# An 8-head attention phase: the last pair's product with the values moved to directly behind the next scores

## The chip, the cores and the metric

The kernel runs on one core of one Trainium2 chip. The metric is the device time of one execution in microseconds (us), taken as the median of several runs. One execution of it was recorded by the profiler, and all rows below come from that trace.

## What is computed

The program is a two-layer decoder on x of 16 batches x 256 rows x 512 features. Each of four steps adds to x: a 16-head cross attention (phase a), a ternary feed-forward step (phase b), an 8-head cross attention with heads of 64 features (phase c), and a routed feed-forward step (phase m). The change lies in phase c alone, whose reference is, cut to its core:

```python
q = layernorm(xn, g, b) @ Wq; k, v = split(media @ Wkv)       # xn: x normalised once more before
q, k, v = heads(q) * 64 ** -0.5, heads(k), heads(v)           # 8 heads of 64
sim = einsum('bhid,bhjd->bhij', q, k)
sim = where(media_mask, sim, neg_inf)
attn = softmax(sim)
out = einsum('bhij,bhjd->bhid', attn, v)
x = x + merge(out) @ Wo
```

## The kernel before, in words

All order is written out by hand: each engine has its own program, and the engines meet only at semaphores. Phase c goes through 16 batches; a batch has two **quads** of four heads (q = 0 and 1), a quad two **pairs** of heads, and a pair is one group of 128 output features. Python names carry the prefix `c_` in the trace. Full-precision products are made of fp32r parts: each operand is split into a high part (written by ScalarE) and a low part (VectorE: the bank minus the high part), and three products are added up.

In one quad TensorE goes through four slots j = 0 to 3:

- T_j: `transpose_probs`, four transposes of the probabilities of head j (L1149) into one bank, which VectorE (even j) or ScalarE (odd j) copies out to `pT`.
- behind T_0 only: `scores` of the *next* quad (L1132, 24 matmuls on 64 rows of the array each).
- behind T_1 the product PV of `probs_v` (L1162) for the last pair of the quad before; behind T_2 the PV of this quad's first pair. It is four fp32 matmuls with 64 columns of weights each, and it shows as eight in the trace. Both write the one bank `o_bank`.
- then the **units** of the slot, from `SLOTS`: pieces of the projections of the next batch, and of the output product (L1079 with `c_wo`) of the batch before. For q = 0 they are [tx0, tx1], [k0], [q0], [o0]; for q = 1 [o1], [k1], [q1 and half of v0], [the rest of v0, v1]. tx0 and tx1 turn the normalised rows of the next batch (L1069, four transposes each), k and q are projections (L1093).

The units share two banks of PSUM in turn: a unit's bank is its place in the list of units modulo 2, and `bank_free` lets it start once the unit before it in the bank is out. tx0 and k0 have the same bank, so k0 waits, beside its other operands, at

```python
            pe.wait_ge(lo_done, units.count(SPLIT, v, ve))     # L1045, here with v = "tx0"
```

for the low part of tx0 (`lo_of`, L810, on VectorE), which itself waits for the high part (`hi_of`, L600, on ScalarE), which waits for tx0's transposes.

ScalarE (`quad_of_8` in `scalar`) takes in turn: the exponentials of the next quad's head 0 (`exps`, L652), the high parts of slot 0, the copy of T_1 (L660), the high part of PV (`attn_hi`, L667), the exponentials of head 1, and so on. VectorE (`quad_of_8` in `vector`) has the copy of T_0 (L855), the score maxima of heads 0 and 1 (`scores_out`, L846), the low parts of slot 0, the maxima of head 2, the low part of PV (`attn_lo`, L881), the maxima of head 3, the copy of T_2.

In the last batch of phase c there are no units for a next batch; in their place the next phase, m, turns its weights (L2519) and its first rows (L2487) in the same slots, with high and low parts again on ScalarE (L2174) and VectorE (L2282). A piece of weight may be turned only once the low part of the piece before the last is out.

Phase a is the same function with 16 heads. There `QUADS` is 4, and its PV stands directly behind `scores` already (`PV_AFTER = {0: -1}`); its scores use 32 rows of the array and its PV 32 columns.

Of the kernel before, what the change touches and what calls it, by code (L numbers as in the profile page):

```python
# [145 lines left out]
def attention_phase(nc, ctx, banks, tag, heads, x_in, ctx_in, mask_in, mask_value, x_out, w_views, q_bias, k_bias,  # L146
# [6 lines left out]
    QUADS = heads // 4  # L153
# [96 lines left out]
    def finished(parts):  # L250

        return [u.rstrip("b") for u in parts if u[-1] != "a"]
# [13 lines left out]
    def quads_left(el, q):  # L266

        return (el.n - batches) * QUADS + q if isinstance(el.n, int) and el.n >= batches - 2 else None
# [7 lines left out]
    def owner(el, u):  # L276

        return el.plus(units.offset(u))

    def exists(el, u):  # L280

        n = el.n
        return not isinstance(n, int) or 0 <= n + units.offset(u) < batches

    def has_before(el):
        return not isinstance(el.n, int) or el.n > 0
# [7 lines left out]
        return "q" + str(q // 2 if QUADS == 4 else q)  # L294


    PV_AFTER = {0: -1} if QUADS == 4 else {1: -1, 2: 0}

    def group_of(el, q, back):

# [14 lines left out]
    def slot_of(q, h):  # L315
        return 2 * (q % 2) + h // 2
# [320 lines left out]
    def scalar(act, beside=None):  # L637

        def hi_of_slot(el, q, j):
            for u in finished(SLOTS[q][j]):  # L640
                if exists(el, u):
                    hi_of(act, owner(el, u), u)
            if beside and QUADS == 2 and quads_left(el, q):
                beside.scalar_slot(act, quads_left(el, q), j)

        def exps(el, q, h):

            s = slot_of(q, h)
            for t in range(QT):
                act.wait_ge(ttr_done, (el.n * heads + 4 * q + h) * QT + t + 1)  # L650
                pr = probs[:, s, h % 2, t]
                nc.scalar.activation(pr, pr, ACT.Exp, bias=negm[:, s, h % 2, t:t + 1], scale=-1.0,  # L652
                                     accum_out=ssum[:, s, QT * (h % 2) + t:QT * (h % 2) + t + 1]) \
                    .then_inc(exp_done, 1)

        def probs_out(el, q, j):

            h = 4 * q + j
            act.wait_ge(pt_done, el.n * heads + h + 1)
            nc.scalar.activation(pT[:, (h // hpg) % 2, h % hpg].rearrange("p t n -> p (t n)"),  # L660
                                 pt_bank[:], ACT.Copy).then_inc(odd_out, 1)

        def attn_hi(el, g):

            act.wait_ge(pv_done, el.n * GROUPS + g + 1)
            if v_bias is None:
                nc.scalar.activation(oT[el.par % OT_SETS][:, HI, g], o_bank[:, 0:SEQ], ACT.Copy).then_inc(othi_done, 1)  # L667
            else:
                nc.scalar.activation(oT[el.par % OT_SETS][:, HI, g], o_bank[:, 0:SEQ], ACT.Identity,
                                     bias=cols[:, BV, g:g + 1]).then_inc(othi_done, 1)  # L670

        def attn_hi_after(el, q, j):
            if j in PV_AFTER:
                ge, g = group_of(el, q, PV_AFTER[j])
                if ge is el or has_before(el):
                    attn_hi(ge, g)

        start = Element(0, 0, batches)
        if prior:
            hi_of(act, start, "q0")  # L680
            hi_of(act, start, "v0")
            exps(start, 0, 0)
            exps(start, 0, 1)
            hi_of(act, start, "v1")
            exps(start, 0, 2)
            exps(start, 0, 3)
            hi_of(act, start, "k1")
            hi_of(act, start, "q1")
        else:
            hi_of(act, start, "tc0")  # L690
            hi_of(act, start, "tc1")
            hi_of_weight(act, "Wk")
            hi_of(act, start, "tx0")
            hi_of(act, start, "tx1")
            hi_of_weight(act, "Wq")
            hi_of(act, start, "k0")
            hi_of_weight(act, "Wv")
            hi_of(act, start, "k1")
            hi_of(act, start, "q0")
            hi_of_weight(act, "Wo")  # L700
            hi_of(act, start, "v0")
            exps(start, 0, 0)
            exps(start, 0, 1)
            hi_of(act, start, "v1")
            exps(start, 0, 2)
            exps(start, 0, 3)
            hi_of(act, start, "q1")

        def quad_of_16(el, q):
            ne, nq = next_quad(el, q)  # L710
            more = nq > 0 or el.has(1)
            if more:
                exps(ne, nq, 0)
            attn_hi_after(el, q, 0)
            hi_of_slot(el, q, 0)
            probs_out(el, q, 1)
            if more:
                exps(ne, nq, 1)
            hi_of_slot(el, q, 1)
            if more:  # L720
                exps(ne, nq, 2)
            hi_of_slot(el, q, 2)
            probs_out(el, q, 3)
            if more:
                exps(ne, nq, 3)
            hi_of_slot(el, q, 3)

        def quad_of_8(el, q):
            ne, nq = next_quad(el, q)
            more = nq > 0 or el.has(1)  # L730
            if more:
                exps(ne, nq, 0)
            hi_of_slot(el, q, 0)
            probs_out(el, q, 1)
            attn_hi_after(el, q, 1)
            if more:
                exps(ne, nq, 1)
            hi_of_slot(el, q, 1)
            if more:
                exps(ne, nq, 2)  # L740
            attn_hi_after(el, q, 2)
            if more:
                exps(ne, nq, 3)
            hi_of_slot(el, q, 2)
            probs_out(el, q, 3)
            hi_of_slot(el, q, 3)

        def iteration(el):
            for q in range(QUADS):
                (quad_of_16 if QUADS == 4 else quad_of_8)(el, q)  # L750
                if beside and quads_left(el, q):
                    beside.scalar_beside(act, quads_left(el, q))

        run_elements(act, batches, iteration)
        attn_hi(Element(0, batches - 1, batches), GROUPS - 1)
# [83 lines left out]
    def vector(dve, beside=None):  # L839

        def scores_out(el, q, h):

            s = slot_of(q, h)
            wait_apart(dve, s_done, (el.n * QUADS + q) * S_SETS + h * S_SETS // 4 + 1)
            for t in range(QT):
                nc.vector.tensor_tensor_reduce(  # L846
                    out=probs[:, s, h % 2, t], in0=s_bank[h][:, t * SEQ:(t + 1) * SEQ],
                    in1=mbias[:, el.par], scale=-sm_scale, scalar=BIG, op0=ALU.add, op1=ALU.min,
                    accum_out=negm[:, s, h % 2, t:t + 1]).then_inc(ttr_done, 1)
# [21 lines left out]
        def lo_of_slot(el, q, j):  # L871
            for u in finished(SLOTS[q][j]):
                if exists(el, u):
                    lo_of(dve, owner(el, u), u)
            if beside and QUADS == 2 and quads_left(el, q):
                beside.vector_slot(dve, quads_left(el, q), j)
# [11 lines left out]
        def attn_lo_after(el, q, j):  # L888
            if j in PV_AFTER:
                ge, g = group_of(el, q, PV_AFTER[j])  # L890
                if ge is el or has_before(el):
                    attn_lo(ge, g)
# [76 lines left out]
        def quad_of_8(el, q):  # L969
            ne, nq = next_quad(el, q)  # L970
            more = nq > 0 or el.has(1)
            probs_out(el, q, 0)
            if q > 0:
                lo_of_slot(el, q - 1, 3)
            elif has_before(el):
                lo_of_slot(el.plus(-1), QUADS - 1, 3)
            if q == 0 and el.has(1):
                mask_bias(dve, el.plus(1))
            if more:
                scores_out(ne, nq, 0)  # L980
                scores_out(ne, nq, 1)
            lo_of_slot(el, q, 0)
            if more:
                scores_out(ne, nq, 2)
            attn_lo_after(el, q, 1)
            if more:
                scores_out(ne, nq, 3)
            probs_out(el, q, 2)
            lo_of_slot(el, q, 1)
            attn_lo_after(el, q, 2)  # L990
            if more:
                recip(ne, nq, 0)
            lo_of_slot(el, q, 2)
            if more:
                recip(ne, nq, 1)
            if q == 0 and el.has(2):
                row_stats(dve, el.plus(2))
# [116 lines left out]
    def tensor(pe, beside=None):  # L1114
# [71 lines left out]
        def iteration(el):  # L1186
            for q in range(QUADS):
                ne, nq = next_quad(el, q)
                for j in range(4):
# [6 lines left out]
                    if j == 0 and beside and QUADS == 4 and quads_left(el, q):  # L1196
                        beside.tensor_totals_read(pe, quads_left(el, q))
                    if j in PV_AFTER:
                        ge, g = group_of(el, q, PV_AFTER[j])
                        if ge is el or has_before(el):  # L1200
# [1596 lines left out]
```

## Time and profile before

| | |
|---|---|
| median of 3 runs | 1976.47 us (1975.31 to 1977.74) |
| the profiled execution, its own time | 1977.67 us |
| its span, first to last instruction | 1975.9 us |
| TensorE busy | 1918.8 us (97% of the span) |
| VectorE, ScalarE, GpSimd busy | 1300.2, 1030.9, 781.6 us |
| mean granted TensorE clock | 0.992 |

Rows of a timeline give the start of a piece, its length, the engine (PE is TensorE, PEld its weight loads, DVE VectorE, ACT ScalarE), the line, what is written from what, and the count. A bracket at the end gives the idle time ahead of the piece on its engine and what ended it. Matmuls overlap in the pipeline, so the length of a piece reaches into the next one; what a piece costs TensorE is the distance from its start to the start of the next.

### The profile page before, as it was taken

To read this page: it belongs to the slowest core of one execution; us is meant where nothing else is said; L and a number is where in the kernel's file an instruction comes from. 1 tells how busy PE (TensorE), PEld (TensorE's weight loads), DVE (VectorE), ACT (ScalarE), POOL (GpSimd) and SP (SyncE) were. 2 spreads that over 40 slices of the span, in tenths; PEclk is the share of its full clock that TensorE was granted. 3 is DMA by queue.
4 is the path that set the end of the run, shared out by engine and by line. 5 is a ranking of instruction groups with operands and counts; after the bars stand their busy time and mean duration, and the time that the engine had idled before them with its cause. 6 is when DMAs were issued, how large, how long until landed. Compare 5 with 4: busy or idle time off the path is not lost.

```text
span 1975.9 us, 43601 instructions
## 1 busy us (share of the span) xinstructions
PE 1918.8 (97%) x13828; PEld 1464.4 (74%) x13860; DVE 1300.2 (66%) x4035; ACT 1030.9 (52%) x2687; POOL 781.6 (40%) x1439
## 2 busy tenths in 40 slices
PE   6999999999999799999999999999999989999998
PEld 5888888888888544444447888888888867787875
DVE  5777777677776677688875565655556566544475
ACT  5777677776777644544444444444444443222252
POOL 2555445554546745455542122221222222222263
PEclk9999999999999999999999999999999999999999
DMA  6332233223325468665542222122121226322131
GB/s 221 122 124 84 83 122 126 83 83 103 145 80 203 147 142 190 165 148 139 138 114 103 77 68 95 54 86 76 66 95 54 86 101 219 100 84 72 64 129 43
DMA packets 197371, 219.01 MB, mean 111 GB/s; under 512 B 105440, under 2 KB 115680, under 8 KB 197232
## 3 DMA queue, kind: packets, MB, share of 16 engines
q1 hardware_dynamic: 197232, 217.41, 35.3%
q8 instruction: 57, 0.93, 0.2%
q14 instruction: 82, 0.67, 0.1%
HBM read 143.95 MB, written 50.35 MB: 98 GB/s over the span
## 4 chain that ended last, share of the span: by engine, by line
PE 90%; DVE 3%; issue 2%; POOL 1%; DMA 1%; ACT 1%; SPq 0%; DVEq 0%; POOLq 0%; ACTq 0%
PE bank L1093 19%; PE bank L1079 18%; PE bank L2581 13%; PE bank L1783 10%; PE bank L1149 8%; PE bank L1162 6%; PE bank L1798 5%; PE bank L1132 5%; PE bank L1069 2%; DMA b_hqT<-b_hq 1%; PE bank L2487 1%; PE bank L2620 1%; POOL b_raw L1480 0%; DVE m_hrow L2418 0%; POOL a_probs L527 0%
## 5 line engine op out<-in xcount | busy, mean ns | idle before, releaser
L527 POOL TENSOR_SCALAR a_probs<-a_probs,a_rinv 128x256 f32<-128x256 f32 x512 | 237.4, 482 | 302.1 <-DVE a_rinv L862 302.1
L652 ACT ACTIVATE a_probs<-a_probs,a_negm 128x256 f32<-128x256 f32 x512 | 254.6, 502 | 113.3 <-DVE a_negm L846 112.6
L527 POOL TENSOR_SCALAR c_probs<-c_probs,c_rinv 128x256 f32<-128x256 f32 x128 | 67.1, 534 | 375.0 <-DVE c_rinv L862 375.0
L846 DVE CUSTOM_DVE_ANT_0 a_probs<-bank,a_mbias 128x256 f32<-128x256 f32 x512 | 191.7, 417 | 5.6 <-PE bank L1132 3.7
L2581 PE MATMUL bank<-m_xnT,m_s 128*128 128x512 f32 x768 | 187.2, 395 | 2.8 <-DVE m_hid L2322 2.8
L855 DVE COPY a_pT<-bank 128x512 f32<-128x512 f32 x128 | 88.2, 689 | 137.5 <-PE bank L1149 137.3
L652 ACT ACTIVATE c_probs<-c_probs,c_negm 128x256 f32<-128x256 f32 x256 | 127.1, 500 | 89.2 <-DVE c_negm L846 89.2
L2581 PEld LDWEIGHTS bank<-m_xnT,m_s 128*128 128x128 f32 x768 | 144.5, 191 | 34.3 <-DVE m_hid L2322 3.3
L1149 PE MATMUL bank<-a_ident,a_probs 128*128 128x128 f32 x1024 | 155.4, 275 | 8.3 <-ACT a_pT L660 4.6
L1149 PEld LDWEIGHTS bank<-a_ident,a_probs 128*128 128x128 f32 x1024 | 122.1, 141 | 26.0 <-issue 8.6
L1783 PE MATMUL bank<-b_wg,b_xqT 128*128 128x512 bf16 x500 | 130.7, 381 | 5.2 <-ACT b_gate L1590 3.6
L1601 ACT ACTIVATE b_hq<-b_hround 128x1024 bf16<-128x1024 f32 x64 | 67.4, 1053 | 123.8 <-POOL b_hround L1533 123.8
L1783 PE MATMUL bank<-b_wu,b_xqT 128*128 128x512 bf16 x502 | 131.0, 381 | 0.5
L1798 PE MATMUL bank<-b_wd,b_hqT 128*128 128x512 bf16 x502 | 117.2, 385 | 2.3 <-DMA b_hqT<-b_hq 1.1
L2111 POOL TENSOR_TENSOR m_hidT<-m_hid,m_hidT 128x512 fp32r<-128x512 f32 x32 | 41.7, 1304 | 196.3 <-ACT m_hidT L2192 196.3
L855 DVE COPY c_pT<-bank 128x512 f32<-128x512 f32 x64 | 43.8, 685 | 110.1 <-PE bank L1149 110.1
L1590 ACT ACTIVATE b_gate<-bank,b_xs 128x512 f32<-128x512 f32 x128 | 86.9, 683 | 52.1 <-PE bank L1783 49.3
L660 ACT ACTIVATE a_pT<-bank 128x512 f32<-128x512 f32 x128 | 76.3, 596 | 71.0 <-PE bank L1149 70.2
L1093 PE MATMUL bank<-a_cT,a_wk 128*128 128x256 f32 x768 | 108.8, 292 | 1.6 <-DVE a_wk L762 1.6
L1697 DVE SCALAR_TENSOR_TENSOR b_hid<-bank,b_xs,b_gate 128x512 f32<-128x512 f32 x128 | 95.5, 747 | 21.8 <-ACT b_gate L1590 17.9
L1093 PE MATMUL bank<-a_xnT,a_wq 128*128 128x256 f32 x768 | 107.0, 289 | 0.0
L1079 PE MATMUL bank<-a_wv,a_cT 128*128 128x512 f32 x384 | 104.0, 407 | 1.2 <-DVE a_wv L762 1.2
(285 smaller groups left out, 4405.9 us busy)
## 6 DMA issues: line engine op xcount, KB each, us to landing
kept<-a_cT SPq DMA_DIRECT2D x32, 512.0 KB, 5.6
m_ew<-in_L_ffn_w_dram SPq DMA_DIRECT2D x24, 512.0 KB, 7.9
a_cbuf<-in_ctx_dram SPq DMA_DIRECT2D x16, 512.0 KB, 6.5
a_xbuf<-in_x_dram SPq DMA_DIRECT2D x16, 512.0 KB, 5.8
a_resb<-in_x_dram SPq DMA_DIRECT2D x16, 512.0 KB, 4.3
x<-a_resb SPq DMA_DIRECT2D x16, 512.0 KB, 2.8
b_xbuf<-x SPq DMA_DIRECT2D x32, 256.0 KB, 2.9
b_resb<-x SPq DMA_DIRECT2D x32, 256.0 KB, 3.3
```

Of the source, the lines that this page charges most:

```text
L527: last = nc.gpsimd.tensor_scalar(pr, pr, rinv[:, s, r:r + 1], 0.0, ALU.mult, ALU.add)
L652: nc.scalar.activation(pr, pr, ACT.Exp, bias=negm[:, s, h % 2, t:t + 1], scale=-1.0, accum_out=ssum[:, s, QT * (h % 2) + t:QT * (h % 2) + ...
L846: nc.vector.tensor_tensor_reduce(out=probs[:, s, h % 2, t], in0=s_bank[h][:, t * SEQ:(t + 1) * SEQ], in1=mbias[:, el.par], scale=-sm_scale ...
L855: nc.vector.tensor_copy(pT[:, (h // hpg) % 2, h % hpg].rearrange("p t n -> p (t n)"), pt_bank[:]) \
L1079: last = nc.tensor.matmul(dst[:], src[:, t * P:(t + 1) * P], w[:, b, k], start=(k == 0 and (a, b) == TERMS[0]), stop=(k == KC - 1 and (a, ...
L1093: last = nc.tensor.matmul(dst[:, m * SEQ:(m + 1) * SEQ], w[:, b, k, f * P:(f + 1) * P], xnT[:, a, k] if u[0] == "q" else turned_context(el ...
L1132: last = nc.tensor.matmul(s_bank[h][:, t * SEQ:(t + 1) * SEQ], qT[el.par][r, a, f, t * P:(t + 1) * P], kT[el.par][r, b, f], start=((a, b) ...
L1149: last = nc.tensor.transpose(pt_bank[:, kt * SEQ + t * P:kt * SEQ + (t + 1) * P], probs[:, s, m, t, kt * P:(kt + 1) * P], ident[:])
L1162: last = nc.tensor.matmul(o_bank[c, 0:SEQ], vb[:, el.par, kt, g * P + m * hd:g * P + (m + 1) * hd], pT[:, g % 2, m, kt], start=(kt == 0), ...
L1783: last = nc.tensor.matmul(bank[c % 2][:], xqT[:, el.par, k], w[:, k, c * DIM:(c + 1) * DIM], start=(k == 0), stop=(k == KC - 1))
L1798: last = nc.tensor.matmul(d_bank[:], hqT[:, el.par, k], wd[:, k], start=(k == 0), stop=(k == IK - 1))
L2581: ins = nc.tensor.matmul(bank[:], *operands(a, b, k), start=(k == 0 and (a, b) == TERMS[0]), stop=(k == KC - 1 and (a, b) == TERMS[-1]))
```

## The change

In phase c the PV of the last pair of the quad before goes from slot 1 (behind T_1) to slot 0 (behind the scores of the next quad, ahead of the slot's units). ScalarE makes its high part ahead of the high parts of slot 0, and VectorE its low part ahead of the low parts of slot 0. Phase a keeps its order.

```diff
-    PV_AFTER = {0: -1} if QUADS == 4 else {1: -1, 2: 0}
+    PV_AFTER = {0: -1} if QUADS == 4 else {0: -1, 2: 0}
...
             if more:
                 exps(ne, nq, 0)
+            attn_hi_after(el, q, 0)
             hi_of_slot(el, q, 0)
             probs_out(el, q, 1)
-            attn_hi_after(el, q, 1)
             if more:
                 exps(ne, nq, 1)
...
                 scores_out(ne, nq, 0)
                 scores_out(ne, nq, 1)
+            attn_lo_after(el, q, 0)
             lo_of_slot(el, q, 0)
             if more:
                 scores_out(ne, nq, 2)
-            attn_lo_after(el, q, 1)
             if more:
                 scores_out(ne, nq, 3)
```

TensorE, a quad q = 0 (here of batch 1), from the scores of the next quad to T_2:

```order
 L1132 MATMUL bank<-c_kT_145,c_qT_143 128x256 x24
+L1162 MATMUL bank<-c_pT,c_vb 64x256 x4
 L1069 MATMUL bank<-c_ident,c_xn 128x128 x8
 L1149 MATMUL bank<-c_ident,c_probs 128x128 x4
-L1162 MATMUL bank<-c_pT,c_vb 64x256 x4
 L1093 MATMUL bank<-c_cT,c_wk 128x256 x24
 L1149 MATMUL bank<-c_ident,c_probs 128x128 x4
```

PV (L1162) now stands between the scores and the transposes of tx0 and tx1 (L1069), and T_1 (L1149) is followed directly by k0 (L1093).

TensorE, the quad q = 1 of the same batch:

```order
 L1149 MATMUL bank<-c_ident,c_probs 128x128 x4
 L1132 MATMUL bank<-c_kT_144,c_qT_142 128x256 x24
+L1162 MATMUL bank<-c_pT,c_vb 64x256 x4
 L1079 MATMUL bank<-c_wo,c_oT_155 128x512 x12
 L1149 MATMUL bank<-c_ident,c_probs 128x128 x4
-L1162 MATMUL bank<-c_pT,c_vb 64x256 x4
 L1093 MATMUL bank<-c_cT,c_wk 128x256 x24
```

Here PV goes ahead of o1 (L1079), and T_1 is followed by k1.

ScalarE, the quad q = 0 of batch 1:

```order
 L595 ACTIVATE c_vb<-bank 128x512 x2
 L652 ACTIVATE c_probs,c_ssum<-c_probs,c_negm 128x256 x2
+L667 ACTIVATE c_oT_155<-bank 128x256
 L600 ACTIVATE c_xnT<-bank 128x4x128 x2
 L660 ACTIVATE c_pT<-bank 128x512
-L667 ACTIVATE c_oT_155<-bank 128x256
 L652 ACTIVATE c_probs,c_ssum<-c_probs,c_negm 128x256 x2
 L607 ACTIVATE c_kT_144<-bank 128x512
```

The high part of PV (L667) goes ahead of the high parts of tx0 and tx1 (L600). On VectorE the low part (L881) goes in the same way from between the maxima of heads 2 and 3 to ahead of the low parts of tx0 and tx1 (L810). GpSimd's and SyncE's instructions are the same. All 32 quads of phase c but the very first have a PV in this place, so 31 are moved.

## Rows read from the trace of the kernel before

**Rows 1.** The page: the chain that ended last, shares of the span by engine.

```profile
PE 90%; DVE 3%; issue 2%; POOL 1%; DMA 1%; ACT 1%; SPq 0%; DVEq 0%; POOLq 0%; ACTq 0%
```

**Rows 2.** Busy time by stretch: one batch, and 14 batches of phase c.

```profile
1265.29:1300.61 35.32, 35.32 (x265) 29.73 (x264) 20.73 (x67) 16.58 (x50) 8.48 (x19) 1.00 0.21 75
...
1089.00:1583.17 494.17, 494.17 (x3695) 415.86 (x3694) 288.79 (x934) 231.92 (x700) 115.32 (x260) 1.00 0.22 76
```

**Rows 3.** Timeline of TensorE, a quad q = 0, T_0 to T_2.

```profile
1265.29 0.60 PE L1149 MATMUL bank<-c_ident,c_probs 128*128 128x128 f32 x4
1265.82 1.70 PE L1132 MATMUL bank<-c_kT,c_qT 64*128 64x256 f32 x24
1267.44 1.09 PE L1069 MATMUL bank<-c_ident,c_xn 128*128 128x128 f32 x8
1268.38 0.60 PE L1149 MATMUL bank<-c_ident,c_probs 128*128 128x128 f32 x4
1268.90 1.08 PE L1162 MATMUL bank<-c_pT,c_vb 128*64 128x256 f32 x8
1269.92 3.14 PE L1093 MATMUL bank<-c_cT_odd,c_wk 128*128 128x256 f32 x24
1272.90 0.60 PE L1149 MATMUL bank<-c_ident,c_probs 128*128 128x128 f32 x4
```

**Rows 4.** Timeline of TensorE in phase a, start and middle.

```profile
28.90 0.98 PE L1132 MATMUL bank<-a_kT,a_qT 32*128 32x256 f32 x24
29.81 3.04 PE L1079 MATMUL bank<-a_wv,a_cT 128*128 128x512 f32 x12
...
305.33 0.98 PE L1132 MATMUL bank<-a_kT,a_qT 32*128 32x256 f32 x24
306.24 1.07 PE L1162 MATMUL bank<-a_pT,a_vb 128*32 128x256 f32 x16
307.24 1.70 PE L1093 MATMUL bank<-a_cT,a_wk 128*128 128x256 f32 x12
308.77 0.60 PE L1149 MATMUL bank<-a_ident,a_probs 128*128 128x128 f32 x4
309.13 1.67 PE L1093 MATMUL bank<-a_cT,a_wk 128*128 128x256 f32 x12
```

**Rows 5.** Timeline, ScalarE and VectorE in the quad of rows 3.

```profile
1268.42 1.06 ACT L600 ACTIVATE c_xnT<-bank 128x512 fp32r<-128x512 f32 x2
1269.03 1.29 DVE L810 TENSOR_TENSOR c_xnT<-bank,c_xnT 128x512 fp32r<-128x512 f32 x2 [0.61 <-ACT c_xnT L600]
...
1270.04 0.39 ACT L667 ACTIVATE c_oT<-bank 128x256 fp32r<-128x256 f32 x1
```

**Rows 6.** Timeline, VectorE and TensorE in batch 0, q = 0.

```profile
1060.26 1.29 DVE L810 TENSOR_TENSOR c_xnT<-bank,c_xnT 128x512 fp32r<-128x512 f32 x2 [0.61 <-ACT c_xnT L600]
...
1061.01 3.13 PE L1093 MATMUL bank<-c_cT_odd,c_wk 128*128 128x256 f32 x24 [0.80 <-DVE c_xnT L810]
```

**Rows 7.** Timeline, TensorE and ScalarE in the last quad of phase c.

```profile
1607.69 1.10 PE L2487 MATMUL bank<-m_ident,m_xn 128*128 128x128 f32 x8 [1.56 <-DVE m_s L2282]
...
1608.39 1.08 ACT L2164 ACTIVATE m_xnT<-bank 128x512 fp32r<-128x512 f32 x2 [1.83 <-PE bank L2487]
```

**Rows 8.** Timeline of TensorE, batch 0, q = 1.

```profile
1070.71 1.69 PE L1132 MATMUL bank<-c_kT,c_qT 64*128 64x256 f32 x24
1073.66 0.63 PE L1149 MATMUL bank<-c_ident,c_probs 128*128 128x128 f32 x4 [1.26 <-DVE c_pT L855]
...
1075.23 3.14 PE L1093 MATMUL bank<-c_cT_odd,c_wk 128*128 128x256 f32 x24
```

**Rows 9.** Timeline of TensorE in the last batch, q = 0.

```profile
1587.80 1.11 PE L2519 MATMUL bank<-m_ident,m_raw 128*128 128x128 f32 x8
...
1591.25 1.17 PE L2519 MATMUL bank<-m_ident,m_raw 128*128 128x128 f32 x8 [0.80 <-DVE m_s L2282]
...
1593.73 3.02 PE L1079 MATMUL bank<-c_wo,c_oT 128*128 128x512 f32 x12 [0.88 <-DVE m_s L2282]
```

## The prediction, made before the run

> **What bounds the kernel now.** I read the page first. The chain that ended last is TensorE for 90% of the span [rows 1]. Phase c is harder still: the busy times by stretch show TensorE at 494.17 of 494.17 us over fourteen batches, each 35.32 us long, with VectorE at 59% (20.73 us) and ScalarE at 47% of a batch, at the full granted clock [rows 2]. There PE has no idle time for an earlier operand to fill. So the time can change in two ways only: the same matmuls follow each other at other distances, or a wait appears. I read the timeline of one quad for the distances, start to start [rows 3]: T_0 0.53, scores 1.62, tx0 and tx1 0.94 together, T_1 0.52, PV 1.02, k0 2.98, in sum 7.61 us from T_0 to T_2.
>
> **The switch that is saved.** T costs 0.52 us when scores or PV come next [rows 3], but 0.36 when a full-array product does (308.77 to 309.13) [rows 4]. So 0.16 to 0.17 us is the price of going from the full array to one cut into parts. Today that is paid twice ahead of T_2, before the scores and before PV. The changed order goes from scores straight to PV, and T_1 is followed by k. What PV costs behind scores in this phase no row shows. Phase a shows the nearest: its scores take 0.91 us whether a full-array product follows (28.90 to 29.81) or PV does (305.33 to 306.24), and PV behind them takes 1.00 [rows 4]. I take that PV behind scores adds no switch of its own: scores 1.62, PV 1.02. The bounds: nothing extra, and a full switch of 0.17. A quad then saves 0.17 us, if nothing waits.
>
> The Trainium skill, "TensorEngine Tiling (Array Packing)", section Tiling Modes, says "Mode switching requires drain". Scores and PV are two different modes there, so by it the count per quad falls from four switches to three. The page has no price. The rows agree that leaving and entering cost something, and by its rule alone every moved PV would be a gain, which is the second rival below.
>
> **The wait that appears in q = 0.** Here PV is put ahead of tx0 and tx1, and T_1 and PV no longer stand together between them and k0. k0 shares its bank with tx0 and waits for tx0's low part. The chain behind tx0, piece by piece:
> - start of tx0's transposes to the start of its high part on an idle ScalarE: 0.70, by 1607.69 to 1608.39, transposes of the same shape that also started with no weights loaded ahead [rows 7];
> - high part to low part: 0.61 (1268.42 to 1269.03) [rows 5];
> - start of the low part to k0: 0.75 (1060.26 to 1061.01), a place where k0 did wait 0.80 us for just this [rows 6].
>
> In sum 2.06 us. Before, tx0 started at 1267.44. ScalarE, held up by its exponentials, took the high part at 1268.42, 0.28 later than it could have. The low part started at 1269.03, so k0 was free at 1269.78, and it started at 1269.92 since PV held TensorE until then [rows 3, 5]. PV was the cover, with 0.14 us to spare. After: tx0 starts one PV later, at 1267.44 + 1.02 = 1268.46, and k0 can start at 1268.46 + 2.06 = 1270.52. TensorE is through with tx0, tx1 and T_1 at 1268.46 + 0.94 + 0.36 = 1269.76 and idles 0.76 us. Queued behind k0 is all else on TensorE, so the idle time is on the path. Against 1269.92 k0 starts 0.60 later. The quad costs 0.60 us more, and with the full switch of 0.17 also on the way 0.77.
>
> The new place of PV's high part on ScalarE does not add to this: it started 1.14 after PV (1268.90 to 1270.04) and took 0.39 [rows 3, 5], so it would end at 1267.44 + 1.53 = 1268.97, ahead of 1269.16 when tx0 is turned. Its low part on VectorE ends by the same distances near 1269.4, ahead of 1269.77. If ScalarE could start 0.1 earlier the price would be 0.5. I take 0.60 with bounds 0.45 and 0.77.
>
> **q = 1.** Slot 0 is o1, an output product that ScalarE has no part in; k1 waits for the output rows of o0, which are written a slot earlier. The 0.17 us is kept. A batch so costs 0.60 - 0.17 = 0.43 us more: the batch length goes from 35.32 to 35.75.
>
> **How many.** Batches 1 to 14 have both kinds: 14 x 0.43 = 6.0 us. Batch 0 has no PV to move in q = 0.
>
> **Start.** In q = 1 of batch 0, scores start at 1070.71 and are through 1.62 later, at 1072.33. TensorE then idles for VectorE's copy of T_0 until T_1 at 1073.66, and T_1, PV and k1 follow, k1 at 1075.23 [rows 8]. PV fits into that hole (1072.33 to 1073.35), so k1 can start at 1073.66 + 0.36 = 1074.0: 1.2 us gained. Nothing later in these two batches waits, so the bounds are 0.2 (the saved switch alone) and 1.3.
>
> **End.** In batch 15 phase m's weights are turned in slots 0 to 2, and TensorE waits there for their low parts: 0.80, 0.88 and 1.56 us [rows 7, 9]. This is a chain over three engines, and PV now delays its first link. The first two pieces turn one PV later, at 1586.34 by the distances above, and the third waits for the low part of the first: 1586.34 + 2.06 = 1588.40 instead of 1587.80 [rows 9]. ScalarE's and VectorE's exponentials and maxima absorb part: I walk the chain on with the same durations and get 0.43 late at the product that started at 1593.73 [rows 9]. In q = 1 there are no scores, so no switch is saved, the pieces again turn one PV later, and the same walk gives 1.0 late at 1607.69 [rows 7]. The walk is an estimate; its bounds are 0 and two PVs, 2.0. I take 1.0.
>
> **Sum.** 6.0 - 1.2 + 1.0 = +5.8 us, 0.29%. The durations are from an execution of 1977.67 us, which becomes 1983.5. That execution lies 1.20 above the median of the three runs, and against the median, 1976.47, the forecast is 1982.3. No instruction, no byte and no DMA is added or removed, and SyncE's and GpSimd's rows are the same; phase m's loads hang on TensorE's progress and move with it.
>
> **The rivals.**
> 1. *The forecast*, k0's wait in every q = 0. For it: the wait is in the code, and rows 6 show it biting when no PV stands between. Own range: q = 0 between 0.45 and 0.75, and start and end inside their bounds, 1979.5 to 1985.
> 2. *k0 does not wait* and only the switches are saved: 28 quads x 0.17 = 4.8 us, with start and end as above 4.8 + 1.2 - 1.0 = 5.0 us faster, 1971.5. For it: TensorE is the bound and the count of switches does fall. Against it: tx0's chain would have to take 1.30 us (0.94 + 0.36) instead of 2.06, and none of its three pieces has a row that short. It decides from a chain under 1.30. Between this and the forecast lies a partial wait: the two kinds of quad cancel when k0 starts 0.17 later than now, with a chain of 1.63.
> 3. *PV behind scores pays a full switch.* All 28 quads are 0.17 dearer, 4.8 us: 1987.1. For it: the 64-row to 64-column case has no row of its own. Against it: phase a pays nothing for 32-row to 32-column.
> 4. *About nothing*: a partial wait of 0.2 to 0.4 us, or a start and an end that both come out well, 1975 to 1980. For it: each of the three pieces was measured at another place than tx0 behind PV.
>
> **How the numbers follow.** Chances: forecast 0.71, rival 2 0.09, rival 3 0.08, rival 4 0.12. A measurement of this kernel tells about 0.2% from no change, that is 4.0 us, so "the same" is 1972.5 to 1980.4. The forecast's own range reaches into it by a small part (0.04) and rival 4 almost whole (0.11). Faster: 0.09. Slower: 0.67 + 0.08 + 0.01 = 0.76. Same: 0.15. The range reaches from 1978.3 to 1987.0: the forecast's 0.71, about half of rival 3 and of rival 4, 0.81.
>
> **What the new profile would show.** The length of a batch is the first test, 35.75 us if all steps hold, 34.98 by rival 2, 36.09 by rival 3. In q = 0: tx0 1.02 us behind PV, T_1 0.94 behind tx0, k0 1.1 us behind T_1 with an idle time near 0.76 put down to VectorE L810, and T_2 8.2 us behind T_0. In q = 1: PV 1.62 behind the scores, T_1 to k1 0.36, no idle time. In the first quads k1 0.36 behind T_1. If T_1 to k0 is 0.36, the chain was wrong; if scores to PV is 1.8, the switch was. The end is right if TensorE's waits for L2282 in the last batch grow by about 1 us in sum.

## The result, and the profile after

| | before | after |
|---|---|---|
| median | 1978.37 us (1975.31 to 1981.04, 20 runs) | 1982.03 us (1979.17 to 1986.9, 20 runs) |
| ratio of the times | | 1.0022, 95% interval 1.0016 to 1.0028 |
| profiled execution, span | 1975.9 us | 1978.2 us |
| phase c, first scores to phase m's first rows (L2487) | 562.86 us | 568.90 us |
| all the rest of the span | 1413.0 us | 1409.3 us |

The changed kernel is slower by 0.22% by this ratio, some 4.3 us; the two medians are 3.7 us apart. I read the busy times by stretch first: one batch from T_0 to T_0, and the fourteen batches from scores to scores. The columns are the stretch and its length, busy time of PE, PEld, DVE, ACT and POOL with counts, granted clock, DMA share and GB/s.

```profile
1265.53:1301.34 35.81, 35.19 (x266) 29.69 (x265) 20.82 (x67) 16.57 (x50) 8.48 (x19) 1.00 0.21 74
1087.26:1587.92 500.66, 492.61 (x3697) 415.66 (x3696) 290.18 (x934) 232.01 (x701) 115.38 (x260) 1.00 0.21 75
```

TensorE was busy for the whole of both stretches before [rows 2]. Now 8.05 us of the fourteen batches are idle, while its busy time fell (the rows of before end at T_0 of batch 15; from scores to scores they are 494.48 us). This batch went from 35.32 to 35.81 us, and the mean of fourteen is 35.76. The waits of TensorE between 1080 and 1580 us are one row: line waited at, who ended it, us in total, times, the longest.

```profile
PE bank L1093 <- DVE c_xnT L810: 8.1, 14, 0.6
```

Fourteen waits, one for each q = 0 of batches 1 to 14. This is the timeline of one such quad, the counterpart of [rows 3, 5].

```profile
1265.53 0.60 PE L1149 MATMUL bank<-c_ident,c_probs 128*128 128x128 f32 x4
1266.06 1.69 PE L1132 MATMUL bank<-c_kT,c_qT 64*128 64x256 f32 x24
1267.68 1.08 PE L1162 MATMUL bank<-c_pT,c_vb 128*64 128x256 f32 x8
1268.70 1.09 PE L1069 MATMUL bank<-c_ident,c_xn 128*128 128x128 f32 x8
1268.82 0.38 ACT L667 ACTIVATE c_oT<-bank 128x256 fp32r<-128x256 f32 x1
...
1269.39 1.08 ACT L600 ACTIVATE c_xnT<-bank 128x512 fp32r<-128x512 f32 x2 [0.19 <-PE bank L1069]
1269.63 0.60 PE L1149 MATMUL bank<-c_ident,c_probs 128*128 128x128 f32 x4
1270.02 1.29 DVE L810 TENSOR_TENSOR c_xnT<-bank,c_xnT 128x512 fp32r<-128x512 f32 x2 [0.37 <-ACT c_xnT L600]
...
1270.85 3.13 PE L1093 MATMUL bank<-c_cT_odd,c_wk 128*128 128x256 f32 x24 [0.62 <-DVE c_xnT L810]
```

The three steps of the chain can be read off as distances of starts: tx0 at 1268.70, its high part 0.69 later, its low part 0.63 later, k0 another 0.83 later. The bracket gives the 0.62 us of TensorE's idle time, put down to VectorE L810. In the next batch k0 follows tx0 by 2.07 instead of 2.15 and idles 0.54: in six of the fourteen, the first half of the loop's body where k0 reads `c_cT_odd`, the wait is 0.62, and in the other eight 0.54.

In q = 1 nothing waits, and T_1 is followed by k1 at 0.35 (1287.56 to 1287.91). The start of phase c shows the gap in which PV now stands: TensorE idles 0.25 us ahead of T_1, against 1.26 before, and k1 starts 3.34 behind the scores, against 4.52 [rows 8].

```profile
1069.97 1.69 PE L1132 MATMUL bank<-c_kT,c_qT 64*128 64x256 f32 x24
1071.59 1.08 PE L1162 MATMUL bank<-c_pT,c_vb 128*64 128x256 f32 x8
1072.92 0.63 PE L1149 MATMUL bank<-c_ident,c_probs 128*128 128x128 f32 x4 [0.25 <-DVE c_pT L855]
1073.31 1.91 PE L1093 MATMUL bank<-c_cT_odd,c_wk 128*128 128x256 f32 x14
```

In the last batch there is a new first wait for a piece of phase m's weights (0.60), two that shrank from 0.80 and 0.88 to 0.56 and 0.80, and the last, 1.56, as before [rows 7, 9]. From T_0 of the batch to L2487 it is 25.59 us instead of 24.52. The waits with a name grew by only 0.28 of these 1.07 us, from 3.24 to 3.52. Most of the rest lies in q = 1 and has no bracket: the second twelve transposes of weights take 1.79 us up to the next piece (1607.63 to 1609.42) instead of 1.47 (1602.65 to 1604.12), and T_1 ahead of them takes 0.71, where up to such transposes it mostly takes 0.43. The second twelve before,

```profile
1602.65 1.53 PE L2519 MATMUL bank<-m_ident,m_raw 128*128 128x128 f32 x12
```

and the last batch after.

```profile
1587.40 0.60 PE L1149 MATMUL bank<-c_ident,c_probs 128*128 128x128 f32 x4
...
1592.69 1.25 PE L2519 MATMUL bank<-m_ident,m_raw 128*128 128x128 f32 x8 [0.60 <-DVE m_s L2282]
...
1595.95 1.16 PE L2519 MATMUL bank<-m_ident,m_raw 128*128 128x128 f32 x8 [0.56 <-DVE m_s L2282]
...
1598.35 3.02 PE L1079 MATMUL bank<-c_wo,c_oT 128*128 128x512 f32 x12 [0.80 <-DVE m_s L2282]
...
1607.63 1.85 PE L2519 MATMUL bank<-m_ident,m_raw 128*128 128x128 f32 x12
...
1612.99 1.10 PE L2487 MATMUL bank<-m_ident,m_xn 128*128 128x128 f32 x8 [1.56 <-DVE m_s L2282]
```

So phase c grew by 6.04 us in the trace, and the span by only 2.3. The missing 3.7 us lie outside the change: phase c began 0.7 us earlier, and phase m was 3.0 us shorter (368.21 to 365.21). Here are the first 60 us of phase m in three stretches, first before,

```profile
1607.69:1627.69 20.00, 17.80 (x94) 13.55 (x95) 9.89 (x23) 7.74 (x13) 6.30 (x17) 0.95 0.11 42
1627.69:1647.69 20.00, 19.25 (x83) 14.63 (x81) 11.49 (x48) 5.91 (x9) 8.15 (x15) 0.96 0.87 287
1647.69:1667.69 20.00, 17.91 (x128) 13.68 (x129) 13.83 (x61) 8.12 (x13) 3.35 (x3) 0.91 0.68 220
```

and after.

```profile
1612.99:1632.99 20.00, 17.71 (x98) 13.44 (x99) 10.25 (x24) 7.80 (x13) 6.30 (x17) 1.00 0.11 38
1632.99:1652.99 20.00, 17.82 (x80) 13.57 (x78) 12.43 (x55) 5.85 (x8) 8.16 (x15) 1.00 0.90 297
1652.99:1672.99 20.00, 19.33 (x141) 14.95 (x142) 14.89 (x59) 8.00 (x13) 3.85 (x3) 1.00 0.78 260
```

The granted clock was 0.91 to 0.96 in the profiled execution of before and 1.00 in that of after. The same 24 matmuls of phase m (L2581) took 6.64 us from start to start at 1626.77 before and 5.55 at 1631.72 after. One pair of executions can't say whether the change has a part in that, so the experiments below are judged by the length of phase c beside the time of the whole.

### The profile page after: what moved, and what is told of

The parts are those of the page before. It is cut to its first block, busy times and chain, and to the rows that moved or that the text cites. A ratio compares the mean times of both kernels' runs of the same rounds, so it can differ in the third digit from the quotient of the medians.

```text
span 1978.2 us, 43633 instructions
## 1 busy us (share of the span) xinstructions
PE 1916.3 (97%) x13860; PEld 1461.0 (74%) x13860; DVE 1301.7 (66%) x4035; ACT 1031.5 (52%) x2687; POOL 781.6 (40%) x1439
## 4 chain that ended last, share of the span: by engine, by line
PE 90%; DVE 4%; issue 2%; ACT 2%; POOL 1%; DMA 1%; SPq 0%; DVEq 0%; POOLq 0%; ACTq 0%
PE bank L1093 19%; PE bank L1079 18%; PE bank L2581 13%; PE bank L1783 10%; PE bank L1149 8%; PE bank L1162 6%; PE bank L1798 6%; PE bank L1132 5%; PE bank L1069 2%; PE bank L2487 1%; DVE c_xnT L810 1%; PE bank L2620 1%; DMA b_hqT<-b_hq 0%; ACT c_xnT L600 0%; DVE m_hrow L2418 0%
## 5 line engine op out<-in xcount | busy, mean ns | idle before, releaser
L2581 PE MATMUL bank<-m_xnT,m_s 128*128 128x512 f32 x768 | 184.7, 392 | 2.8 <-DVE m_hid L2322 2.8
L2581 PEld LDWEIGHTS bank<-m_xnT,m_s 128*128 128x128 f32 x768 | 142.6, 188 | 33.6 <-DVE m_hid L2322 3.3
L1149 PE MATMUL bank<-a_ident,a_probs 128*128 128x128 f32 x1024 | 154.9, 274 | 7.9 <-ACT a_pT L660 4.2
L1149 PEld LDWEIGHTS bank<-a_ident,a_probs 128*128 128x128 f32 x1024 | 121.7, 141 | 25.5 <-issue 8.1
L1093 PE MATMUL bank<-a_cT,a_wk 128*128 128x256 f32 x768 | 109.9, 295 | 1.6 <-DVE a_wk L762 1.6
L1093 PE MATMUL bank<-a_xnT,a_wq 128*128 128x256 f32 x768 | 107.1, 289 | 0.0
L1093 PEld LDWEIGHTS bank<-a_cT,a_wk 128*128 128x128 f32 x768 | 98.0, 195 | 10.0 <-issue 6.2
```

Source lines behind the costliest of these rows:

```text
L1093: last = nc.tensor.matmul(dst[:, m * SEQ:(m + 1) * SEQ], w[:, b, k, f * P:(f + 1) * P], xnT[:, a, k] if u[0] == "q" else turned_context(el ...
L1149: last = nc.tensor.transpose(pt_bank[:, kt * SEQ + t * P:kt * SEQ + (t + 1) * P], probs[:, s, m, t, kt * P:(kt + 1) * P], ident[:])
L2581: ins = nc.tensor.matmul(bank[:], *operands(a, b, k), start=(k == 0 and (a, b) == TERMS[0]), stop=(k == KC - 1 and (a, b) == TERMS[-1]))
```

## The experiments

The theory: TensorE bounds phase c. The change saves one entry into split mode (0.17 to 0.19 us) in each quad. But it turns tx0 one PV (1.02) later, and k0 waits for the bank of tx0 until that chain of 2.07 to 2.15 us is over. The start gains 1.2 us and the last batch loses 1.07. Rivals: PV's high and low parts, now ahead of tx0's on ScalarE and VectorE, delay them; the loss lies in q = 1 or in the last batch; the gain in q = 1 is not the switch but k1's place right behind T_1; what is measured is the variation of the other phases.

All nine, in one table. Batch is the mean of batches 1 to 14, T_0 to T_0 or scores to scores; phase c is from its first scores to phase m's first rows; rest is the remainder of the same span.

| kernel | batch | phase c | rest | ratio to before, 95% interval |
|---|---|---|---|---|
| before | 35.32 | 562.86 | 1413.0 | |
| changed | 35.76 | 568.90 | 1409.3 | 1.0022 (1.0016 to 1.0028) |
| e7_changed_again | 35.76 | 568.99 | 1412.8 | 1.0036 (1.0023 to 1.0049) |
| e1_q1_only | 35.13 | 559.07 | 1414.6 | 0.9985 (0.9977 to 0.9994) |
| e2_q0_only | 35.95 | 571.72 | 1411.7 | 1.0044 (1.0031 to 1.0057) |
| e3_last_kept | 35.76 | 567.87 | 1410.8 | 1.0023 (1.0011 to 1.0035) |
| e4_parts_late | 35.76 | 569.28 | 1416.0 | 1.0034 (1.0021 to 1.0047) |
| e6_behind_units | 35.23 | 560.35 | 1408.4 | 0.9985 (0.9974 to 0.9996) |
| e5_rows_first | 35.02 | 557.42 | 1410.6 | 0.9969 (0.9957 to 0.9980) |
| e9_rows_first_again | 35.02 | 557.40 | 1409.6 | 0.9957 (0.9943 to 0.9970) |
| e8_one_row_first | 34.94 | 556.37 | 1413.5 | 0.9965 (0.9951 to 0.9979) |

### One half of the change at a time

```diff
-    PV_AFTER = {0: -1} if QUADS == 4 else {0: -1, 2: 0}
+    def early(el, q):
+        return q == 1 and not last_batch(el)
+
+    def pv_after(el, q, j):
+        if QUADS == 4:
+            return {0: -1}.get(j)
+        return {(0 if early(el, q) else 1): -1, 2: 0}.get(j)
```

ScalarE and VectorE take PV's parts in the place that goes with it. The second kernel has `q == 0` in `early`.

> PV goes behind the scores in q = 1 only (and not in the last batch); q = 0 and the last batch are as before. Nothing is left out of the computation. Theory (the change loses in q = 0 alone, where k0 waits for tx0's low part, and gains a switch of 0.19 us in every q = 1, 20.00 to 19.81, and 1.2 us at the start of phase c): a batch takes 35.32 - 0.19 = 35.13 us, q = 0 stays at 15.32, k0 shows no idle time, and the kernel is 14 x 0.19 + 1.2 = 3.9 us faster than before, ratio 0.998. Rival (PV behind the scores costs something wherever it stands, by its parts being ahead of the slot's parts on ScalarE and VectorE): q = 1 at or above 20.0 and no gain against before.

> PV goes behind the scores in q = 0 only, the last batch kept as before. Nothing is left out of the computation. Theory: q = 0 is 0.60 to 0.68 us longer (15.92 to 16.00), q = 1 stays 20.00, a batch 35.95 on average, phase c 8 x 0.60 + 6 x 0.68 = 8.9 us longer than before, ratio 1.0045; k0 waits 0.54 to 0.62 us for VectorE L810. Rival (the loss of the changed kernel comes from q = 1 or from the last batch): a time near before, ratio under 1.001.

Measured: with q = 1 alone a batch takes 35.13, phase c is 3.79 us shorter than before and the kernel faster, 0.9985. With q = 0 alone a batch takes 35.95, phase c is 8.86 us longer, 1.0044. The q = 1 of the first kernel, TensorE:

```profile
1280.71 1.70 PE L1142 MATMUL bank<-c_kT,c_qT 64*128 64x256 f32 x24
1282.34 1.08 PE L1172 MATMUL bank<-c_pT,c_vb 128*64 128x256 f32 x8
1283.35 3.02 PE L1089 MATMUL bank<-c_wo,c_oT 128*128 128x512 f32 x12
1286.21 0.60 PE L1159 MATMUL bank<-c_ident,c_probs 128*128 128x128 f32 x4
1286.57 3.11 PE L1103 MATMUL bank<-c_cT_odd,c_wk 128*128 128x256 f32 x24
```

Scores to PV is 1.63, PV 1.01, T_1 0.36, and no row has an idle time. The second kernel has the fourteen waits of 0.54 and 0.62, and no other that the kernel before doesn't have. The halves add up, as two parts that don't touch each other do: -3.79 + 8.86 + 1.07 for the last batch = 6.14, and the whole change measured 6.04 and 6.13. (The gain of 1.2 at the start belongs to q = 1 and is in the first term.) The loss is q = 0.

### The last batch kept, and the change once more

```diff
     def early(el, q):
-        return q == 1 and not last_batch(el)
+        return not last_batch(el)
```

That is the first; the second is the changed kernel unaltered.

> The change everywhere but in the last batch, which is as before. Nothing is left out of the computation. Theory (in the last batch PV stands ahead of phase m's weight pieces, and the chain piece, low part, next piece but one is later by 1.07 us at phase m's first rows): T_0 of the last batch to the first rows of phase m takes 24.52 us as before, against 25.59 with the change; phase c is 568.90 - 1.07 = 567.8 us from its first scores to there, 5.0 over before; the time is 1.1 us under the changed kernel's. Rival (the later end came from the batches before, through loads or ScalarE's backlog): 25.4 or more there.

> The changed kernel itself, unaltered, as the partner of the other two on the same chip. Theory: phase c takes 568.9 us from its first scores to phase m's first rows again, within 0.4, and what differs from the first profile lies in phases a, b and m; ratio against before 1.0022 to 1.003. Rival (what phase c takes varies from one execution to the next by as much as the whole kernel's time): over 1 us off 568.9.

Measured: 567.87 and 568.99 us of phase c. With the last batch kept, T_0 to the first rows takes 24.51 us (1590.30 to 1614.81), and its waits are those of before, 0.80, 0.89 and 1.56:

```profile
1590.30 0.60 PE L1159 MATMUL bank<-c_ident,c_probs 128*128 128x128 f32 x4
...
1598.38 1.17 PE L2530 MATMUL bank<-m_ident,m_raw 128*128 128x128 f32 x8 [0.80 <-DVE m_s L2293]
...
1614.81 1.10 PE L2498 MATMUL bank<-m_ident,m_xn 128*128 128x128 f32 x8 [1.56 <-DVE m_s L2293]
```

The end of phase c costs 1.1 us and is made in the last batch. The changed kernel's phase c repeats within 0.1 us, while the rest of its span went from 1409.3 to 1412.8.

### PV's high and low parts back where they were

```diff
-            attn_hi_after(el, q, 0)
             hi_of_slot(el, q, 0)
             probs_out(el, q, 1)
+            attn_hi_after(el, q, 0)
...
-            attn_lo_after(el, q, 0)
             lo_of_slot(el, q, 0)
             if more:
                 scores_out(ne, nq, 2)
+            attn_lo_after(el, q, 0)
```

> TensorE's order is that of the changed kernel, but the high part of PV on ScalarE stands behind the copy of T_1 again, and its low part on VectorE between the maxima of heads 2 and 3, as before the change. Nothing is left out of the computation. Theory (what is late is tx0's own chain, since PV stands ahead of it on TensorE; ScalarE and VectorE are done with PV's parts before tx0 is turned): q = 0 stays at 15.92 to 16.00, the idle time ahead of k0 stays within 0.1 of 0.54 to 0.62, the kernel is within 0.1% of the changed one, ratio 1.0015 to 1.003 against before. Rival (PV's two parts, now ahead of tx0's parts, delay them): k0's wait goes, q = 0 takes 15.32 - 0.17 = 15.15 us, a batch 34.96, ratio 0.997.

Measured: a batch 35.76, the waits of k0 unchanged. ScalarE now has nothing ahead of tx0's high part for 0.64 us, and the chain is no shorter:

```profile
1275.14 1.09 PE L1069 MATMUL bank<-c_ident,c_xn 128*128 128x128 f32 x8
1275.84 1.09 ACT L600 ACTIVATE c_xnT<-bank 128x512 fp32r<-128x512 f32 x2 [0.64 <-PE bank L1069]
...
1276.47 1.29 DVE L810 TENSOR_TENSOR c_xnT<-bank,c_xnT 128x512 fp32r<-128x512 f32 x2 [1.37 <-ACT c_xnT L600]
...
1277.30 3.13 PE L1093 MATMUL bank<-c_cT_odd,c_wk 128*128 128x256 f32 x24 [0.62 <-DVE c_xnT L810]
```

From tx0 to k0 it is 2.16, against 2.15. The rival of the parts falls: in batches 1 to 14 their place costs nothing and gives nothing, and only TensorE's order matters. In the last batch it does matter: from T_0 to phase m's first rows it takes 25.92 us instead of 25.59. There the late high part of PV (0.40 us) stands on ScalarE ahead of head 1's exponentials, the high part of the next piece of weight starts 6.62 us behind T_0 instead of 6.35, and TensorE's second wait for L2282 is 0.80 instead of 0.56.

### PV in slot 0, but behind the units

On top of the kernel with the last batch kept and the parts late:

```diff
+                    behind = QUADS == 2 and j == 0 and early(el, q)
+                    if behind:
+                        use_slot(el, q, j)
                     back = pv_after(el, q, j)
...
-                    use_slot(el, q, j)
+                    if not behind:
+                        use_slot(el, q, j)
```

> PV stays in slot 0, but behind the slot's units and ahead of T_1, with its two parts where they were before the change; the last batch is as before. Nothing is left out of the computation. T_1 is followed by k0 and k1 as with the change, but PV does not stand behind the scores, so the same number of switches as before is made, and tx0 is turned as early as before. Theory (the gain is the adjacency of scores and PV, the loss tx0's lateness): no idle time ahead of k0, q = 0 15.32, q = 1 20.00, a batch 35.32 as before, and only the start gains about 1.1 us: ratio 0.9995. Rival (the gain in q = 1 comes from k1 standing right behind T_1, not from the switch): q = 1 at 19.8, a batch at 34.9 to 35.0, ratio 0.997. Second rival (k0 waits for something else than tx0's chain): its idle time of 0.54 to 0.62 stays, a batch near 35.9.

Measured: no idle time ahead of k0, a batch 35.23, between theory (35.32) and first rival (34.9 to 35.0) but nearer the theory; phase c is 2.51 us shorter, of which the batches give 1.3 and the start 1.2. TensorE in q = 0 of this kernel:

```profile
1263.97 1.69 PE L1142 MATMUL bank<-c_kT,c_qT 64*128 64x256 f32 x24
1265.60 1.09 PE L1079 MATMUL bank<-c_ident,c_xn 128*128 128x128 f32 x8
1266.62 1.08 PE L1172 MATMUL bank<-c_pT,c_vb 128*64 128x256 f32 x8
1267.64 0.66 PE L1159 MATMUL bank<-c_ident,c_probs 128*128 128x128 f32 x4
1268.05 3.12 PE L1103 MATMUL bank<-c_cT_odd,c_wk 128*128 128x256 f32 x24
```

The second rival falls: with tx0 as early as before, the wait is gone. The first falls in its size: k1 behind T_1 does not bring the 0.17 when PV stands apart from the scores (q = 1 is 19.96 here, 20.00 before and 19.81 with the change). But my price of a switch was too simple, since it compares what follows. Four transposes of T take 0.36 us up to a full-array product and 0.52 up to scores or PV, which is the 0.17. Up to further transposes, where the array is not cut either, they take 0.43 (T_0 to tx0, in both sets of rows of the next experiment). So PV behind tx1 costs only 0.08 (1.02 for tx0 and tx1 instead of 0.94), which is the step from 0.43 to 0.52. T_1 right behind PV costs 0.41 instead of 0.36, and k0 takes 2.95 up to T_2 instead of 2.98 behind PV. With the same number of switches as before, q = 0 is so 0.06 us shorter and q = 1 0.04.

### tx0 and tx1 ahead of the scores

If only the distance from tx0 to k0 matters, it can be made longer from the other side. On top of the kernel with the last batch kept:

```diff
+    def tx_first(el, q):
+        return QUADS == 2 and q == 0 and has_before(el) and not last_batch(el)
...
+                    if tx_first(el, q) and j == 0:
+                        use_slot(el, q, 0)
                     if j == 0 and (nq > 0 or el.has(1)):
                         scores(ne, nq)
```

On ScalarE their high parts go ahead of the exponentials of head 0, on VectorE their low parts ahead of the maxima. The third kernel of this kind moves tx0 alone and leaves tx1 behind PV, on the three engines alike:

```diff
+    def ahead(el, q):
+        return ["tx0"] if QUADS == 2 and q == 0 and has_before(el) and not last_batch(el) else []
...
+                    for u in ahead(el, q) if j == 0 else ():
+                        use(pe, owner(el, u), u)
                     if j == 0 and (nq > 0 or el.has(1)):
                         scores(ne, nq)
```

> In q = 0 of batches 1 to 14 the units tx0 and tx1 go ahead of the scores (with their high and low parts at that place on ScalarE and VectorE), PV stays behind the scores, and the last batch is as before the change. Nothing is left out of the computation. Theory (only the distance from tx0 to k0 matters, and each switch saved is worth 0.17 to 0.19): scores and PV, 2.6 us together, now stand between tx1 and T_1, so tx0's chain of 2.07 is over before k0, which shows no idle time; q = 0 takes 15.32 - 0.17 = 15.15, q = 1 19.81, a batch 34.96, and the kernel is 14 x 0.36 + 1.2 = 6.2 us faster than before, ratio 0.997. It would lose against that if tx0, tx1 wait for operands or a bank at their new place, up to 0.9 us a batch by the one slot that they are earlier. Rival (the switch saved is not real in q = 0, or k0 waits for something else than tx0's low part): q = 0 at 15.3 or above, ratio 1.0.

> The variant with tx0 and tx1 both ahead of the scores, unaltered, as the partner of the one with tx0 alone on the same chip. Nothing is left out of the computation. Theory: phase c takes 557.4 us again within 0.3 and a batch 35.02, whatever the whole kernel's time does; ratio against before 0.996 to 0.998. Rival (the gain of its first run was the variation of phases a, b and m between executions): ratio not below 0.999.

> In q = 0 of batches 1 to 14 tx0 alone goes ahead of the scores (its high and low parts too), tx1 stays behind PV; the last batch is as before the change. Nothing is left out of the computation. Theory (k0 waits for tx0's chain alone, and in the variant with both units ahead tx1 also waited a little for the bank of v1, which was copied out only about 0.6 us before): k0 shows no idle time, T_0 to T_2 takes 7.61 - 0.17 = 7.44 us against 7.51 with both ahead, a batch 34.95, phase c 562.86 - 14 x 0.37 - 1.2 = 556.5 us, ratio 0.9965 to 0.997. Rival (the 0.06 to 0.07 us that the variant with both ahead fell short was no wait, but the price of T_1 right behind PV and of scores behind transposes): 7.5 us again, a batch 35.0. Second rival (tx1's own place matters: q0 now waits for tx1's low part): an idle time ahead of q0 of 0.2 or more.

Measured: phase c is 5.44 and 5.46 us shorter than before with both ahead, and 6.49 with tx0 alone; the whole kernel is at 0.9969, 0.9957 and 0.9965, medians of 1969.93, 1968.89 and 1970.72 us. All three beat both kernels. First both ahead (the first run of it), q = 0:

```profile
1263.64 0.60 PE L1168 MATMUL bank<-c_ident,c_probs 128*128 128x128 f32 x4
1264.07 1.14 PE L1088 MATMUL bank<-c_ident,c_xn 128*128 128x128 f32 x8
1265.14 1.69 PE L1151 MATMUL bank<-c_kT,c_qT 64*128 64x256 f32 x24
1266.76 1.08 PE L1181 MATMUL bank<-c_pT,c_vb 128*64 128x256 f32 x8
1267.78 0.66 PE L1168 MATMUL bank<-c_ident,c_probs 128*128 128x128 f32 x4
1268.19 3.12 PE L1112 MATMUL bank<-c_cT_odd,c_wk 128*128 128x256 f32 x24
```

Then tx0 alone:

```profile
1265.50 0.60 PE L1166 MATMUL bank<-c_ident,c_probs 128*128 128x128 f32 x4
1265.93 0.60 PE L1086 MATMUL bank<-c_ident,c_xn 128*128 128x128 f32 x4
1266.46 1.70 PE L1149 MATMUL bank<-c_kT,c_qT 64*128 64x256 f32 x24
1268.09 1.08 PE L1179 MATMUL bank<-c_pT,c_vb 128*64 128x256 f32 x8
1269.10 0.66 PE L1086 MATMUL bank<-c_ident,c_xn 128*128 128x128 f32 x4
1269.60 0.60 PE L1166 MATMUL bank<-c_ident,c_probs 128*128 128x128 f32 x4
1269.95 3.12 PE L1110 MATMUL bank<-c_cT_odd,c_wk 128*128 128x256 f32 x24
```

In both k0 follows without an idle time. T_0 to k0 is 4.55 us with both ahead and 4.45 with one. Of that tenth, 0.06 is T_1 behind PV (0.41 against 0.35) and 0.04 the two pieces themselves (1.07 against 0.53 + 0.50). In the trace of both ahead the transposes start 0.11 us apart, but twice 0.16 at the beginning of tx1, so that is where the 0.04 lie. Whether this is a short wait for v1's bank no row says, so theory and first rival of the last kernel both hold in part. Its second rival falls: q0 does not wait. By the time of the whole kernel the three runs are not told apart; by phase c, tx0 alone is 1.0 us better.

## Why the prediction was right

**What bounds the kernel** was read rightly: every change of TensorE's distances in the fourteen batches showed up in phase c at its full size.

**The wait of k0.** Predicted were idle 0.76, k0 1.1 behind T_1 and T_0 to T_2 8.2. Measured are k0 1.22 (and 1.14) behind T_1, T_0 to T_2 8.29 (and 8.20), idle 0.62 (and 0.54). The chain was put at 2.06 and took 2.15 and 2.07: 0.70 was 0.69, 0.61 was 0.63, 0.75 was 0.83. The idle time is less than 0.76 although k0 is no earlier, because a record of four transposes lasts 0.60 while they cost 0.36 until the next start; the idle time ought to have been stated from the record's end. The price against before, 0.60, was 0.60 in eight quads and 0.68 in six. In those six the last step took 0.83, not 0.75, so PV had covered the chain with 0.06 us to spare (1269.03 + 0.83 against 1269.92), not 0.14. That ScalarE and VectorE would be done with PV's parts in time held, and the kernel with late parts shows it.

**The saved switch.** Taken as 0.17 in q = 1, measured 0.19 (20.00 to 19.81 us from scores to scores). Scores to PV is 1.62 and PV 1.02, the value taken, and the bound of a further 0.17 did not come up. "Mode switching requires drain" (the Trainium skill, "TensorEngine Tiling (Array Packing)", section Tiling Modes) puts four switches ahead of T_2 before and three after, and q = 1 did get shorter. But the switch that remains by that count, from scores to PV, two tiled modes, shows no price in these rows: 1.62 is also what scores cost when a full-array product follows. Nor is all of the 0.17 shown to be the cut of the array: T takes 0.43 and not 0.36 also where transposes of the full array follow.

**The sum.** Batches: predicted +6.0, measured 500.66 - 494.48 = +6.2. Start: -1.2, measured -1.18 from scores to k1 (4.52 to 3.34) and -1.22 from scores to scores. End: +1.0, measured +1.07, and removed by keeping the last batch. In sum +5.8 was predicted, and phase c grew by 6.04 in one execution and 6.13 in another. The walk along the last batch was an estimate and came out close; its midpoint can be checked too: the product after the third piece was to be 0.43 late, and it stands 10.95 us behind T_0 (1587.40 to 1598.35) instead of 10.56, 0.39 late. The sign named for the end did not come true, though: TensorE's waits for L2282 were to grow by about 1 us and grew by 0.28. The size of the end held, but 0.68 of its 1.07 came in q = 1, for the most part as longer distances between pieces of weight without a named wait, and the walk was right there only in its sum.

**The whole.** 1982.3 against a median of 1982.03. That is closer than it deserves: the forecast stood on three runs of before with a median of 1976.47, and twenty gave 1978.37. Against that +5.8 would be 1984.2. The measured difference is 0.22% (0.16 to 0.28) in one comparison and 0.36% (0.23 to 0.49) in the other, and phase c's growth is 0.31% of the time; the first interval just misses that. The rest of the span ran from 1408.4 to 1416.0 us over the eleven profiled executions, with no order in what was changed. Whole executions of the changed kernel differ with their mean granted clock: the four at 0.995 or 0.996 took 1979.17 to 1979.96 us, the five at 0.992 took 1984.40 to 1986.9. That spread is larger than the change itself, and in the pair compared above early phase m is where the clocks differed. Why the clock differs, and whether the change has a part in it, stays open.

**The rivals.** That k0 does not wait (5.0 us faster) was refuted by its fourteen waits. But its arithmetic was sound: without the end's loss of 1.0 its gain is 6.0 us, and where tx0 is turned early enough and the last batch is kept, phase c is 5.4 to 6.5 us shorter. A full switch behind the scores was refuted by the 1.62. A partial wait did not occur.

## What to carry to other kernels

Where a bank is handed over through a chain of engines, a piece of work between the writer and the next user of the bank is cover, and moving it away costs what the chain is longer than what remains: here a PV of 1.02 us had kept a chain of 2.1 us covered with only 0.06 to 0.15 to spare. Before moving it, look whether the chain's head can move ahead too; that turned a loss of 0.2 to 0.4% into a gain of 0.3 to 0.4%. And where differences are of this size, compare the length of the changed phase from the trace as well as the time of the whole: it repeated within 0.1 us in the two pairs of equal kernels, while the rest differed by 3.4 and 1.0 us.

## What the runs showed of the hardware

- Four transposes take 0.52 to 0.53 us up to scores or PV, 0.43 up to further transposes and 0.36 up to a full-array product. The price of cutting the array so depends on what it is compared with: 0.17 us against the product, 0.08 to 0.09 against transposes. Transposes right behind PV cost 0.05 to 0.06 more than behind a full-array product.
- After the start of the same low part k0 started 0.83 us later in one half of the loop's body and 0.74 in the other (1305.83 to 1306.57). No run tells why.
- In the first 60 us of phase m the granted clock was 0.91 to 0.96 in one execution and 1.00 in another, with 3.0 us between them over the whole of phase m. TensorE was busy for 54.96 and 54.86 us of the 60, so its busy time does not tell the two apart.
